# A Fourier image tokenizer before transformer blocks on one Trainium2 core: two scalings written ahead of an inverse root, and image and weight loads requested at other places

## The chip, the cores and the metric

The kernel runs on one core of a Trainium2 chip. The metric is device time in microseconds, lower is better. The engines that matter here are TensorE (PE in the profile, PEld its weight loads), VectorE (DVE), ScalarE (ACT), GpSimd (POOL) and SyncE (SP). SyncE does no arithmetic in this kernel: it waits for semaphores and requests DMA transfers, one after the other.

## The reference

64 images of 64x64 pixels with 3 channels go through a tokenizer, and the 64x64 result of every image through two small transformer blocks. The change touches only the tokenizer:

```
h = layer_norm(x @ fc0_w + fc0_b, ln0_g, ln0_b)          # 3 -> 32 channels
for i in range(4):
    x1 = spectral_conv(h, w1[i], w2[i])                  # rfft2, 2 x 12 x 12 modes mixed, irfft2
    x2 = einsum('bchw,oc->bohw', h, conv_w[i]) + conv_b[i]
    h = layer_norm(x1 + x2, ln_g[i], ln_b[i])            # over the 32 channels
    if i < 3: h = gelu(h)
h = gelu(h @ fc1_w + fc1_b); h = gelu(h @ fc2_w + fc2_b) # 32 -> 128 -> 64
return (h @ fc3_w + fc3_b)[..., 0]                       # 64 -> 1
```

After it come attention, a gated feed-forward net, a linear recurrence and a mixture of experts on the 64x64 hidden state. Neither the kernel before nor the changed one differs there.

## The kernel before, in words

**The loops.** The 64 images go through the tokenizer in 4 groups of 16 (`GROUPS`), and a group in 2 units (`u`) of 8 images. In a group there are five stages: stage 0 is the embedding, stages 1 to 3 are a hardware loop over layers (`l`), stage 4 is the last layer, and then comes the token head (`mlp`, fc1 to fc3). Each engine runs its own program over the same order, and semaphores tie them. Every stage and unit has one *main part*, so there are 4 x 5 x 2 = 40 of them: 8 embedding, 24 layer and 8 last ones. Behind the main part of stages 0 to 3 comes a *forward part* (`pe_forward`: transform along rows and columns, then the mixing with the weights in `mixw`).

**A main part** has 16 chunks of 512 columns. For chunk c, TensorE fills one of six PSUM banks (`wide`: four of `main`, two of `aux`) in L447 or in L454 and L457 and raises `main_full`. In the layers it does this for pairs of chunks: L454 writes the inverse transform of chunks c and c+1, and each needs its bank to be free, that is the scaling (`main_free`) of the chunk six before. ScalarE squares the bank (L730), VectorE sums the squares over the 32 channels (L708, `ssum`), 1/sqrt of the variance is made, and VectorE scales the bank with it into `xn` (L699, the function `scale`). TensorE transposes `xn` (L465, five chunks behind the filling, `LAG`), ScalarE applies gain, bias and GELU (L742), and in the layers TensorE and ScalarE turn the result once more (L473, L748).

**The inverse root** of a pair of chunks is made on VectorE by nine small dependent instructions (`newton_steps`, L659 to L676) for chunks 0 and 1, 2 and 3, 6 and 7, 10 and 11, 14 and 15, and on GpSimd by a power for the others (L762, L765). VectorE's program for a main part sums chunk c, then scales chunk c-3, then may do a Newton chain. `wait_rstd` is the wait for the root of the chunk that is to be scaled.

**SyncE's order** in one group is written by hand: wait for the start value of `main_full`, the images of both units (`sp_x`, 8 transfers and one of the embedding weights per unit, into `yd`), the spectra of both units (`sp_spectrum`: 8 stores to `y_scratch`, a wait for them, one load into `yd`), in the layer loop the next mixing weights (`sp_mixw`, 4.6 MB, one transfer) and two spectra, the first layer's mixing weights for the next group, and the stores of the tokens (`sp_tok`, 8 per unit), each behind the end of its unit's token head.

`yd` holds first a unit's images and later its spectrum. At a group's start TensorE waits for `x_in` before it transposes the images (`pe_embed`, L409), and VectorE and ScalarE wait for all token stores of the group before (`tok_out`, in `drain_embed`) before they copy those transposes out (L598); then TensorE starts the embedding main part (L447).

Of the kernel before, what the change touches and what calls it, by code (L numbers as in the profile page):

```python
# [15 lines left out]
LAYERS, M1, M2 = 4, 12, 12  # L16
GROUP, UNITS = 16, 2
GROUPS = IMGS // GROUP
# [5 lines left out]
NCH = S // 4  # L24
# [14 lines left out]
CHUNKS_GROUP = STAGES * UNITS * NCH  # L39
VAR_STEPS = {4: 3, 5: 3, 8: 3, 9: 3, 12: 2, 13: 2}  # L40

START = 1
# [65 lines left out]
def tokenizer(nc, t, tok, named):  # L108
# [9 lines left out]
    with ctx:  # L118
# [274 lines left out]
        def after(n, c, depth):  # L393

            return n + max(0, c - depth + 1)
# [297 lines left out]
        def dve_main(dve, g, s, u, l, nxt):  # L693
            m, _ = base_of(g, s, u, l)

            def scale(d):
                wait_rstd(dve, m, d)
                dve.wait_ge(tp_full, after(m, d, 2))
                dve.tensor_tensor(xn[:, d % 2, :].rearrange("p (n c) -> p n c", c=CH),  # L699
                                  wide[d % 6][:, :].rearrange("p (n c) -> p n c", c=CH),  # L700
                                  rstd[:, d % 4, :].unsqueeze(2).to_broadcast([128, 16, CH]),
                                  ALU.mult).then_inc(main_free, 1)

            for c in range(NCH):
                dve.wait_ge(sq_full, m + c + 1)
                if c >= 4:
                    wait_rstd(dve, m, c - 4)
                dve.tensor_reduce(ssum[:, c % 4, :], sq[:, c % 2, :].rearrange("p (n c) -> p n c", c=CH), AX.X,  # L708
                                  ALU.add).then_inc(red_done, 1)
                if c >= 3:  # L710
                    scale(c - 3)
                if c % 4 == 3 or c == 1:
                    dve_newton(dve, m, c)
            for d in range(NCH - 3, NCH):
                scale(d)
                if nxt is not None:
                    drain_inverse(dve, 0, g, *nxt, 2 * (d - NCH + 3))
            if nxt is not None:
                drain_inverse(dve, 0, g, *nxt, 6)
# [70 lines left out]
        def sp_x(sp, g, u):  # L790
            for b in range(NB):
                for a in range(NA):
                    img = g * GROUP + (u * UIMG + b * NA + a)
                    sp.dma_start(xb_of(u)[b:128:2, :].rearrange("r (k a n) -> r a k n", k=8, a=NA)[:, a],
                                 t["x"][bass.ds(img, 1)].rearrange("a r (k w) c -> r (a k) (w c)", k=8)).then_inc(x_in[u], 16)

            sp.dma_start(embw_of(u), embw_scratch).then_inc(x_in[u], 16)

        def sp_spectrum(sp, g, s, u, l):
            fwd = (g * (LAYERS * UNITS) + (0 if s == 0 else l * UNITS + UNITS) + u)  # L800
            sp.wait_ge(y_ready, fwd + 1)
            for half in range(2):
                for ro, ri, src in ((0, 0, ys), (0, 1, yn), (1, 0, ys), (1, 1, ys)):
                    part = ri if ro == 0 else 1 - ri
                    rows = 64 * half + 32 * part
                    dst = y_scratch[u].rearrange("(f x r o s m) -> f r s o x m", f=2, x=M1, r=2, o=CH, s=2)[half, ri, ro]
                    sp.dma_start(dst, src[rows:rows + 32, :].rearrange("o (x m) -> o x m", x=M1)).then_inc(y_stored, 16)
            sp.wait_ge(y_stored, fwd * 128 + 144)
            sp.dma_start(yd[0:96, u * YC:(u + 1) * YC], y_scratch[u].rearrange("(p n) -> p n", p=96)).then_inc(yd_in[u], 16)

        def sp_mixw(sp, layer):

            sp.dma_start(mixw[:, :], mix_scratch[bass.ds(layer, 1)].rearrange("a p n -> (a p) n")).then_inc(mixw_in, 16)
# [20 lines left out]
        with nc.Block() as block:  # L834
            @block.tensor
            def _(pe):
                def embed(g):
                    for u in range(UNITS):
                        nxt = (0, 0) if u == 1 else None
                        pe_embed(pe, g, u)  # L840
                        pe_main(pe, g, 0, u, None, nxt)
                        pe_forward(pe, g, 0, u, None, nxt)

                def layer(g, l):
                    for u in range(UNITS):
                        nxt = (1, l) if u == 0 else (0, l + 1)
                        pe_main(pe, g, 1, u, l, nxt)
                        pe_forward(pe, g, 1, u, l, nxt)

                def last(g):  # L850
                    for u in range(UNITS):
                        pe_main(pe, g, LAYERS, u, None, (1, LAYERS - 1) if u == 0 else None)

                def mlp(g):
                    for u in range(UNITS):
                        pe_mlp(pe, g, u)

                program(pe, embed, layer, last, mlp)

            def drains(eng, j, main_of, mlp_of):  # L860
                def embed(g):
                    for u in range(UNITS):
                        drain_embed(eng, j, g, u)
                        main_of(eng, g, 0, u, None, (0, 0) if u == 1 else None)
                        drain_forward(eng, j, g, 0, u, None)

                def layer(g, l):
                    for u in range(UNITS):
                        main_of(eng, g, 1, u, l, (1, l) if u == 0 else (0, l + 1))
                        drain_forward(eng, j, g, 1, u, l)  # L870

                def last(g):
                    for u in range(UNITS):
                        main_of(eng, g, LAYERS, u, None, (1, LAYERS - 1) if u == 0 else None)

                def mlp(g):
                    for u in range(UNITS):
                        mlp_of(eng, g, u)

                program(eng, embed, layer, last, mlp)  # L880

            @block.vector
            def _(dve):
                dve.memset(xs[:, :], 0.0).then_inc(xs_zero, 1)
                for i, counter in enumerate((*aux_full, *aux_free, *inv_full, *inv_free, *row_full, *row_free, turn_full, turn_free, main_full, main_free, sq_full, red_done, var_done, rstd_done, newton, early,
                                             tp_full, tp_free, fc1_full, g1_done, fc2_full, g2_done)):
                    dve.memset(start[:, i:i + 1], 0.0).then_inc(counter, START)
                dve.wait_ge(xs_zero, 1)
                drains(dve, 0, dve_main, dve_mlp)

            @block.scalar
            def _(act):
                for k in range(4):
                    act.wait_ge(p_store[k], 64 * LAYERS)
                act.dma_start(mixw[:, :], mix_scratch[0]).then_inc(mixw_in, 16)
                act.wait_ge(xs_zero, 1)
                drains(act, 1, act_main, act_mlp)

            @block.gpsimd
            def _(pool):  # L900
                def one(s):
                    def f(g, l=None):
                        for u in range(UNITS):
                            pool_main(pool, g, s, u, l)
                    return f
                program(pool, one(0), one(1), one(LAYERS), lambda g: None)

            @block.sync
            def _(sp):

                sp.dma_start(start_scratch[0:1, :], eps[0:1, :]).then_inc(y_stored, 16)
                sp.dma_start(start_scratch[1:2, :], eps[0:1, :]).then_inc(tok_out, 16)
                with sp.Fori(0, GROUPS) as g:

                    sp.wait_ge(main_full, g * CHUNKS_GROUP + START)
                    for u in range(UNITS):
                        sp_x(sp, g, u)
                    for u in range(UNITS):
                        sp_spectrum(sp, g, 0, u, None)
                    with sp.Fori(0, LAYERS - 1) as l:  # L920
                        for u in range(UNITS):
                            if u == 0:
                                sp_mixw(sp, l + 1)
                            sp_spectrum(sp, g, 1, u, l)
                    sp_mixw(sp, 0)
                    for u in range(UNITS):
                        sp_tok(sp, g, u)
                sp.wait_ge(tok_out, GROUPS * UNITS * TOK_DMAS * 16 + 16)
                sp.wait_ge(mixw_in, (GROUPS * LAYERS + 1) * 16)


N_SMALL = 16 + NA * (1 + 2 + 2 * LAYERS + 1) + 4
# [760 lines left out]
```

## Time and profile before

| | us |
|---|---|
| median of 3 runs (lowest, highest) | 4879.39 (4878.88, 4888.92) |
| the profiled execution, its own time | 4884.81 |
| its span in the trace | 4883.0 |
| PE busy | 3992.8 (82% of the span) |
| DVE busy | 2321.4 (48%) |
| ACT busy | 2100.9 (43%) |
| POOL busy | 809.0 (17%) |

A share of busy time is a mean over parts with different limits: preparation of the mixing weights until about 198 us, the four groups until about 4090 us, and the blocks behind them. A gap in square brackets in a row of the timeline is idle time of that engine before the row, with the instruction that ended it.

### The profile page before, as it was taken

What the parts mean: (1) busy time and instruction counts of PE and PEld (TensorE: products, weight loads), DVE (VectorE), ACT (ScalarE), POOL (GpSimd) and SP (SyncE); (2) the same over time, 40 slices, a digit from 0 to 9 for tenths busy, and PEclk for the clock granted to TensorE, in tenths of its full rate; (3) what the DMA queues carried; (4) which work ended last, traced back from release to release, by engine and by line L of the source; (5) the groups of instructions that cost most, each with busy time, mean ns of one, the idle gap of its engine ahead of it and who ended that gap; (6) DMA issues with size and microseconds to landing.
All of it is one profiled execution on the core that took longest, in us unless ns stands there. A gap on an engine that the chain in (4) does not pass through costs nothing. (4 is left out here: it accounts for less than half of the span.)

```text
span 4883.0 us, 102255 instructions
## 1 busy us (share of the span) xinstructions
PE 3992.8 (82%) x39344; PEld 3051.8 (62%) x39344; DVE 2321.4 (48%) x5028; ACT 2100.9 (43%) x3178; POOL 809.0 (17%) x540
## 2 busy tenths in 40 slices
PE   0189999996899999868999999699999995867268
PEld 0068788842687878427888783278888732753146
DVE  6554444531544445225444442244445422777666
ACT  1154444465544444654454446544444473221113
POOL 0031221310212112112121221112212210000020
PEclk9989999998899999989999999799999997778679
DMA  9501202200022021000210210002112101000000
GB/s 205 162 22 60 79 21 64 75 1 16 21 71 69 21 76 63 1 16 21 79 60 21 79 60 2 15 21 79 60 28 72 60 2 31 1 1 1 0 1 9
DMA packets 168694, 213.38 MB, mean 44 GB/s; under 512 B 156402, under 2 KB 158679, under 8 KB 159874
## 3 DMA queue, kind: packets, MB, share of 16 engines
q1 hardware_dynamic: 166514, 182.84, 12.8%
q10 hardware_dynamic: 1680, 23.60, 2.0%
q8 instruction: 347, 5.69, 0.5%
q14 instruction: 153, 1.25, 0.1%
HBM read 147.28 MB, written 59.12 MB: 42 GB/s over the span
## 5 line engine op out<-in xcount | busy, mean ns | idle before, releaser
L765 POOL TENSOR_TENSOR rstd<-var,mhalf 128x16 f32<-128x16 f32 x240 | 698.4, 2910 | 38.8 <-POOL var L762 17.1
L742 ACT ACTIVATE h<-tp,gb 128x512 f32<-128x512 f32 x640 | 554.0, 868 | 303.9 <-PE tp L465 301.9
L708 DVE TENSOR_REDUCE ssum<-sq 128x16 f32<-128x512 f32 x640 | 432.6, 683 | 453.7 <-ACT sq L730 451.3
L762 POOL TENSOR_TENSOR var<-ssum,eps 128x16 f32<-128x16 f32 x240 | 52.0, 217 | 3146.9 <-DVE ssum L708 3146.9
L457 PEld LDWEIGHTS main<-convw,h 128*128 128x128 f32 x3072 | 416.1, 213 | 164.8 <-issue 164.8
L465 PE MATMUL tp<-ident,xn 128*128 128x128 f32 x2560 | 438.7, 299 | 85.5 <-DVE xn L699 80.8
L730 ACT ACTIVATE sq<-main 128x512 f32<-128x512 f32 x480 | 286.4, 599 | 464.0 <-PE main L457 417.4
L506 PE MATMUL main<-fwd_w,pix 128*128 128x96 f32 x4096 | 464.8, 276 | 7.0 <-ACT pix L598 7.0
L506 PEld LDWEIGHTS main<-fwd_w,pix 128*128 128x128 f32 x4096 | 459.8, 192 | 10.3 <-DVE pix L598 8.7
L457 PE MATMUL main<-convw,h 128*128 (+1 forms) x3072 | 465.6, 304 | 0.0
L465 PEld LDWEIGHTS tp<-ident,xn 128*128 128x128 f32 x2560 | 324.1, 154 | 179.6 <-DVE xn L699 141.8
L424 PE MATMUL aux<-inv_r,yd 96*48 96x64 f32 x8192 | 420.0, 256 | 7.1 <-DVE zq L598 4.1
L424 PEld LDWEIGHTS aux<-inv_r,yd 96*48 96x48 f32 x8192 | 388.9, 185 | 46.3 <-issue 34.9
L454 PE MATMUL main<-zq,inv_w 48*128 48x512 f32 x768 | 290.1, 684 | 104.9 <-DVE xn L699 65.5
L699 DVE TENSOR_TENSOR xn<-main,rstd 128x512 f32<-128x512 f32 x480 | 326.9, 682 | 9.4 <-PE tp L465 9.4
L598 DVE COPY t_w<-main 128x384 f32<-128x384 f32 (+1 forms) x192 | 94.2, 491 | 473.5 <-PE main L506 392.7
L598 ACT COPY t_w<-main 128x384 f32<-128x384 f32 (+1 forms) x192 | 81.5, 425 | 505.8 <-PE main L506 405.2
L473 PE MATMUL tp<-ident,h 128*128 128x128 f32 x1536 | 240.0, 280 | 0.0
L748 ACT COPY pix<-tp 128x512 f32<-128x512 f32 x384 | 221.3, 576 | 19.2 <-PE tp L473 19.2
L598 DVE COPY zq<-aux 112x512 f32<-112x512 f32 x128 | 88.2, 689 | 265.5 <-PE aux L424 265.5
L573 PE MATMUL main<-h,f1w 32*128 32x512 f32 x1024 | 182.1, 672 | 14.1 <-ACT pix L773 9.6
L539 PE MATMUL main<-xs,mixw 128*64 128x32 f32 x6144 | 188.9, 223 | 0.0
(240 smaller groups left out, 5952.5 us busy)
## 6 DMA issues: line engine op xcount, KB each, us to landing
mixw<-mix_scratch SPq DMA_DIRECT2D x16, 4608.0 KB, 18.0
y_scratch<-t_w SPq DMA_DIRECT2D x256, 144.0 KB
yd<-y_scratch SPq DMA_DIRECT2D x32, 1152.0 KB, 7.3
mix_scratch<-mixw SPq DMA_DIRECT2D x64, 288.0 KB, 4.8
mixw<-mix_scratch ACTq DMA_DIRECT2D x1, 4608.0 KB, 13.8
h<-in_L_tok_w1r ACTq DMA_DIRECT2D x6, 576.0 KB, 9.7
h<-in_L_tok_w1i ACTq DMA_DIRECT2D x6, 576.0 KB, 10.1
h<-in_L_tok_w2r ACTq DMA_DIRECT2D x6, 576.0 KB, 18.6
```

The source lines that it names most:

```text
L424: mm = pe.matmul(aux[j][64 * half:64 * half + 48, 64 * i:64 * i + 64], ydv[:, u, 8 * e + i, :, :, a].rearrange("p s n -> p (s n)"), inv_r[ ...
L454: pe.matmul(wide[(c + half) % 6][:, :], inv_w[rows, :], zq[rows, 256 * c:256 * c + 512], start=True, stop=False)
L457: mm = pe.matmul(bank[:, 128 * i:128 * i + 128], h[:, (u * S + 4 * c + i) * 128:(u * S + 4 * c + i) * 128 + 128], convw[:, layer, :] if l ...
L465: mm = pe.transpose(tp[0 if turns else d % 2][:, 128 * i:128 * i + 128], xn[:, d % 2, 128 * i:128 * i + 128], ident[:, :])
L473: mm = pe.transpose(tp[1][:, 128 * i:128 * i + 128], h[:, (u * S + 4 * d + i) * 128:(u * S + 4 * d + i) * 128 + 128], ident[:, :])
L506: mm = pe.matmul(main[j][:, 48 * i:48 * i + 96], pv[:, c0 + i, 2 * ap:2 * ap + 2, :].rearrange("p a r -> p (a r)"), fwd_w[:, :], start=Tru ...
L598: return eng.tensor_copy(out, in_) if j == 0 else eng.copy(out, in_)
L699: dve.tensor_tensor(xn[:, d % 2, :].rearrange("p (n c) -> p n c", c=CH), wide[d % 6][:, :].rearrange("p (n c) -> p n c", c=CH), rstd[:, d ...
L708: dve.tensor_reduce(ssum[:, c % 4, :], sq[:, c % 2, :].rearrange("p (n c) -> p n c", c=CH), AX.X, ALU.add).then_inc(red_done, 1)
L730: act.activation(sq[:, c % 2, :], wide[c % 6][:, :], ACT.Square, scale=CH ** -0.5 / (CUBIC if c % 4 >= 2 or c < 2 else 1)).then_inc(sq_ful ...
L742: act.activation(out, in_, fn, bias=gb[:, 1, stage:stage + 1] if l is None else gb[:, 1, bass.ds(stage, 1)], scale=gb[:, 0, stage:stage + ...
L765: pool.tensor_tensor(rstd[:, c % 4, :], var[:, c % 4, :], mhalf[:, :], ALU.pow).then_inc(rstd_done, 2)
```

## The change

In VectorE's program the scalings of chunks 0 and 1 stand directly behind the sums of chunks 2 and 3. Before, they stood behind the sums of chunks 3 and 4. All later scalings stand where they stood.

In SyncE's program the images of group g+1 and the first layer's mixing weights for it are requested when the last main part of group g has filled its last bank, ahead of the token stores. The images of group 0 are requested without a wait. The mixing weights of layer l+1 are requested when the first unit's main part has filled eight banks. The last group requests neither images nor first mixing weights for a group to come.

```
-                if c >= 3:
+                if c in (2, 3):
+                    scale(c - 2)
+                if c >= 5:
                     scale(c - 3)
                 if c % 4 == 3 or c == 1:
                     dve_newton(dve, m, c)
...
-                with sp.Fori(0, GROUPS) as g:
-
-                    sp.wait_ge(main_full, g * CHUNKS_GROUP + START)
-                    for u in range(UNITS):
-                        sp_x(sp, g, u)
+
+                def layers(g):
                     for u in range(UNITS):
                         sp_spectrum(sp, g, 0, u, None)
                     with sp.Fori(0, LAYERS - 1) as l:
                         for u in range(UNITS):
                             if u == 0:
+                                sp.wait_ge(main_full, base_of(g, 1, 0, l)[0] + NCH // 2)
                                 sp_mixw(sp, l + 1)
                             sp_spectrum(sp, g, 1, u, l)
+                    sp.wait_ge(main_full, g * CHUNKS_GROUP + (START + CHUNKS_GROUP))
+
+                for u in range(UNITS):
+                    sp_x(sp, 0, u)
+                with sp.Fori(0, GROUPS - 1) as g:
+                    layers(g)
+                    for u in range(UNITS):
+                        sp_x(sp, g + 1, u)
                     sp_mixw(sp, 0)
                     for u in range(UNITS):
                         sp_tok(sp, g, u)
+                layers(GROUPS - 1)
+                for u in range(UNITS):
+                    sp_tok(sp, GROUPS - 1, u)
                 sp.wait_ge(tok_out, GROUPS * UNITS * TOK_DMAS * 16 + 16)
-                sp.wait_ge(mixw_in, (GROUPS * LAYERS + 1) * 16)
+                sp.wait_ge(mixw_in, GROUPS * LAYERS * 16)
```

VectorE's row at the start of a main part, before: the sums of chunks 2 and 3, the scaling of chunk 0, the first and last step of the Newton chain for chunks 2 and 3, and what follows it.

```order
L708 TENSOR_REDUCE ssum<-sq 128x16 [waits sq_full] x2
L699 TENSOR_TENSOR xn<-main,rstd 128x512 [waits tp_full,rstd_done]
L659 TENSOR_SCALAR var<-ssum 128x32 [waits red_done]
...
L676 SCALAR_TENSOR_TENSOR rstd<-newton_w,rstd 128x32 [waits newton]
L705 REGISTER_ALU
L708 TENSOR_REDUCE ssum<-sq 128x16 [waits rstd_done,sq_full]
L699 TENSOR_TENSOR xn<-main,rstd 128x512 [waits tp_full,rstd_done]
L708 TENSOR_REDUCE ssum<-sq 128x16 [waits rstd_done,sq_full]
L691 REGISTER_ALU
L699 TENSOR_TENSOR xn<-main,rstd 128x512 [waits tp_full,newton]
```

The same place in the changed kernel.

```order
L708 TENSOR_REDUCE ssum<-sq 128x16 [waits sq_full]
L699 TENSOR_TENSOR xn<-main,rstd 128x512 [waits tp_full,rstd_done]
L708 TENSOR_REDUCE ssum<-sq 128x16 [waits sq_full]
L699 TENSOR_TENSOR xn<-main,rstd 128x512 [waits tp_full,rstd_done]
L659 TENSOR_SCALAR var<-ssum 128x32 [waits red_done]
...
L676 SCALAR_TENSOR_TENSOR rstd<-newton_w,rstd 128x32 [waits newton]
L705 REGISTER_ALU
L708 TENSOR_REDUCE ssum<-sq 128x16 [waits rstd_done,sq_full] x2
L691 REGISTER_ALU
L699 TENSOR_TENSOR xn<-main,rstd 128x512 [waits tp_full,newton]
```

The scaling of chunk 0 moved ahead of one sum. That of chunk 1 moved ahead of the whole Newton chain and of one sum. From the scaling of chunk 2 on, the order is the same.

SyncE's row from the end of the layer loop to the tokens of unit 0, before:

```order
L920 REGISTER_ALU
L920 COMPARE_AND_BRANCH
L813 DMA mixw<-mix_scratch 128x9216
L818 ISA
L823 ISA [waits aux_free1,aux_free0]
L823 DMA tok<-pix 16x4x64
```

The same place in the changed kernel, with the repeated image transfers left out.

```order
L919 REGISTER_ALU
L919 COMPARE_AND_BRANCH
L925 ISA
L796 ISA [waits main_full]
L796 DMA yd<-in_x 64x8x24
...
L799 DMA yd<-embw_scratch 97x1024
L815 DMA mixw<-mix_scratch 128x9216
L820 ISA
L825 ISA [waits aux_free1,aux_free0]
L825 DMA tok<-pix 16x4x64
```

The 16 image transfers and two transfers of embedding weights, which before began the next turn of the group loop behind the token stores, now stand ahead of them, behind a wait for `main_full`.

## Rows read from the trace of the kernel before

**Rows 1.** The waits of the whole span: engine, line, releaser, us, times, longest.

```profile
PE aux L409 <- DMA yd<-embw_scratch: 152.2, 4, 55.7
```

**Rows 2.** Timeline of SP's requests at a group's end: start, us, queue, transfer, count.

```profile
1104.31 7.05 SPq L823 DMA_DIRECT2D tok<-pix  x8
1166.17 6.79 SPq L823 DMA_DIRECT2D tok<-zq  x8
1173.69 5.85 SPq L794 DMA_DIRECT2D yd<-in_x  x8
...
1180.26 19.54 SPq L794 DMA_DIRECT2D yd<-in_x  x8
```

**Rows 3.** Timeline of PE: last chunk of the group, then the next group's start.

```profile
1027.74 1.06 PE L457 MATMUL main<-convw,h 128*128 128x128 f32 x8
...
1197.70 1.94 PE L409 MATMUL aux<-ident,yd 128*96 128x128 f32 x8 [32.58 <-DMA yd<-embw_scratch]
1200.50 5.50 PE L447 MATMUL main<-yd 97*128 97x512 f32 x8 [0.86 <-ACT yd L598]
```

**Rows 4.** Timeline of ACT at the same group's start.

```profile
1174.65 1.28 ACT L598 ACT_TABLE_LOAD   x1 [10.74 <-DMA tok<-zq]
1199.68 0.58 ACT L598 COPY yd<-aux 96x512 f32<-96x512 f32 x1 [23.75 <-PE aux L409]
```

**Rows 5.** The waits of SP's queue, whole span.

```profile
SPq L794 <- DVE start L887: 4.7, 1, 4.7
```

**Rows 6.** Timeline of PE, first layer main part of group 0.

```profile
411.16 0.66 PE L465 MATMUL tp<-ident,xn 128*128 128x128 f32 x4 [0.85 <-DVE xn L699]
...
414.87 1.31 PE L454 MATMUL main<-zq,inv_w 48*128 48x512 f32 x2 [2.01 <-DVE xn L699]
...
421.26 1.13 PE L454 MATMUL main<-zq,inv_w 48*128 48x512 f32 x4
...
430.97 1.13 PE L454 MATMUL main<-zq,inv_w 48*128 48x512 f32 x4
```

**Rows 7.** Timeline of DVE, same main part.

```profile
409.23 1.28 DVE L708 TENSOR_REDUCE ssum<-sq 128x16 f32<-128x512 f32 x2
...
411.02 0.17 DVE L659 TENSOR_SCALAR var<-ssum 128x32 f32<-128x32 f32 x1
...
414.14 0.68 DVE L699 TENSOR_TENSOR xn<-main,rstd 128x512 f32<-128x512 f32 x1
...
415.33 0.68 DVE L699 TENSOR_TENSOR xn<-main,rstd 128x512 f32<-128x512 f32 x1
...
425.45 0.68 DVE L699 TENSOR_TENSOR xn<-aux,rstd 128x512 f32<-128x512 f32 x1
```

**Rows 8.** Timeline of ACT and POOL, same main part.

```profile
412.02 1.28 ACT L742 ACT_TABLE_LOAD   x1 [0.82 <-PE tp L465]
...
413.31 0.78 ACT L742 ACTIVATE h<-tp,gb 128x512 f32<-128x512 f32 x1
...
414.80 2.91 POOL L765 TENSOR_TENSOR rstd<-var,mhalf 128x16 f32<-128x16 f32 x1 [0.22 <-POOL var L762]
```

**Rows 9.** Windows: stretch, length, PE PEld DVE ACT POOL busy, PEclk, DMA, GB/s.

```profile
415.70:419.10 3.40, 3.40 (x15) 2.99 (x15) 0.56 (x2) 0.60 (x1) 3.18 (x3) 0.50 0.86 369
...
501.10:507.80 6.70, 6.70 (x28) 5.58 (x27) 1.92 (x4) 2.00 (x4) 5.43 (x3) 0.50 0.18 46
```

**Rows 10.** Idle time of PE before line L454, whole span: releaser, us, times.

```profile
  DVE xn L699: 67.6, 42
```

**Rows 11.** Timeline of DVE, chunk 7 of an embedding main part.

```profile
1297.38 0.69 DVE L708 TENSOR_REDUCE ssum<-sq 128x16 f32<-128x512 f32 x1 [1.16 <-ACT sq L730]
```

**Rows 12.** Mixing weights: landing (the page), one request, first use by PE.

```profile
mixw<-mix_scratch SPq DMA_DIRECT2D x16, 4608.0 KB, 18.0
...
410.02 0.38 SPq L813 DMA_DIRECT2D mixw<-mix_scratch  x1
...
479.26 0.42 PE L539 MATMUL main<-xs,mixw 128*64 128x32 f32 x8
```

## The prediction

> **What bounds the kernel now.** I read the list of waits first, to see what TensorE stands still for. Its largest entry that this change touches is the wait for images at the start of a group: 152.2 us in four times, the longest, at the very start, 55.7 us [rows 1]. The other three make about 32 us each. Then I read the timelines of SyncE, TensorE and ScalarE around one such place, and last the timelines of all engines through the first 20 us of one layer main part. There the reader is to see two things: from chunk 8 on TensorE has hardly a gap, so the main part goes at TensorE's pace, but at its beginning TensorE stands still for the scalings of chunks 0 and 1. The idle time before L454, which needs the scaling of chunk 1 for its second bank, is 67.6 us in 42 times [rows 10]; at 2.01 us a time [rows 6] the 32 layer and last main parts make 64 of it.
>
> **Images ahead of the tokens.** Now SyncE requests the tokens of unit 1 at 1166.17, is through at 1172.96, and only then begins with images. TensorE's transposes start at 1197.70 after 32.58 us idle, and the embedding proper at 1200.50, when ScalarE's copy is out [rows 2 to 4]. In the changed kernel the images are requested when the last chunk is in its bank, near 1029 [rows 3]. One unit took 24.0 us from request to transposes (1173.69 to 1197.70); the second's requests alone lasted 19.5 us. I give both 50 us and the weights 18 us [rows 12]: all has landed before 1104.31, when the first token stores go out [rows 2]. So SyncE's tokens are not late either. What is late next is the wait for the token stores in `drain_embed`: it ended at 1174.65, where ScalarE then loaded a table for 1.28 us before its copy [rows 4]. TensorE's transposes, 1.94 us, fit in the idle time before it. So the copy runs from 1175.95 to 1176.53, and the embedding starts 0.24 us later (1200.50 less the end of the copy, 1200.26), at 1176.77. That is 23.7 us earlier, three times: **71 us**.
>
> At the very start SyncE waited 4.7 us for VectorE's start values [rows 5], and TensorE waited for the images. That wait is gone, but the images then run longer beside the first load of mixing weights. Between 0 and 4.7 us I take **3 us**, nearer to the upper end, since TensorE waits for nothing else there.
>
> **Mixing weights in mid-loop.** One load takes 18.0 us. The request moves from 410.02 to about 417, and the first use is at 479.26 [rows 12]: 44 us of slack, in which the main part's second half and the transforms lie. Cost 0. Without that cover it would be 18 us twelve times. The load for a fifth group, which goes away, was hidden by other work: 0. Behind the new waits on SyncE stand only spectra that become ready later in the same stage.
>
> **Scalings of chunks 0 and 1.** I replay the main part of [rows 6 to 8] with its own durations. VectorE starts a sum or a scaling every 0.60 us when nothing is missing, and the Newton chain of chunks 2 and 3 runs from 411.02 to the sum of chunk 4 at 413.54, 2.52 us. New order: sum 2 at 409.23, scaling 0 at 409.83, sum 3 at 410.42, scaling 1 at 411.02 instead of 414.14, chain 411.62 to 414.14, sums 4 and 5 at 414.14 and 414.74, scaling 2 at 415.33. The work is the same, so scaling 2 stands where it stood. The price of the edit is that sum 4 is 0.6 us later, and with it GpSimd's root of chunk 4.
>
> TensorE: first transposes at 410.57 (was 411.16), L454 for both banks by 411.76 (was 414.87), chunk 6 done near 413.2. The transposes of chunk 1 then wait for ScalarE, which does its squares, loads the GELU table 1.28 us and activates 0.78 us: until 413.9. Chunk 7 is done at 415.85, chunk 2's transposes wait for scaling 2 until 416.3, and the next pair of L454 starts near 417.3. It was 421.26: 3.9 us. Not all of it stays. GpSimd's power takes 2.91 us and now ends near 418.3, so scaling 4 cannot start before 418.35; then comes the chain of chunks 6 and 7, and scaling 5 follows at about 422.1. It was at 425.45 [rows 7]: **3.3 us**. From there on the cycle of four chunks on VectorE (eight times 0.60 and 2.5 to 2.7 us, about 7.5) is shorter than TensorE's 9.7 (421.26 to 430.97 [rows 6]), so the lead stays to the end.
>
> The stall also costs clock. Behind it TensorE's granted clock is 0.50, its lower level of 1.2 GHz, for 3.4 us in this main part, and for 6.7 us in the next one [rows 9]. With only short waits left I expect that the clock does not fall there. In the replay the first 3.4 us are in; where it lasts twice as long, 1.1 to 1.7 us more come back. I take the mean of 3.3 and 4.4 us, 3.85, for 32 main parts: **123 us**.
>
> In the embedding VectorE itself sets the pace, and only its idle before the sum of chunk 7, 1.16 us [rows 11], can shrink. The later GpSimd root leaves 0.6 of it: eight times, **5 us**.
>
> A rule on the table: in 12 main parts (layer loop, first unit) it is loaded between the first scaling and the first activation, and in the new order TensorE waits for it. The rows show the activation at 413.31, directly behind a load of 1.28 us from 412.02 [rows 8]. By the Trainium skill, "ScalarE: Activation LUTs", What ACT_TABLE_LOAD costs, a switch costs 2.66 us with the drain; by that, 1.4 us more would be exposed twelve times and the sum would be 17 us smaller. The row shows no drain of that length before the activation, and the row decides.
>
> **The sum.** 71 + 3 + 123 + 5 = 202 us off the profiled execution's own time of 4884.8, which is 4682.8. The median of the runs is 5.4 us below that execution, so I predict 4678 us.
>
> **The rivals.** *Only the bare idle comes back.* The later sum 4 and GpSimd's root could hold VectorE so that of each of 32 main parts only the 2.01 us before L454 return. For it: these roots do come 0.6 us later. Against it: the replay has that in. It gives 64 + 71 + 3 = 138 us off, 4741 us. Chance 0.12.
>
> *The reordering does nothing.* Scaling 2 does not move, and if all of TensorE's order hung on it, only the loads would pay: 74 us, 4805 us. Against it: TensorE has eight matmuls of chunk 6 and more to do before it needs scaling 2. Chance 0.04.
>
> *The boundary keeps its wait.* If the token stores landed later behind the backlog of loads, or code for the next turn of the loop came late, up to 71 us would stay: 4749 us. Against it: 62 us lie between the two units' tokens [rows 2], with nothing else queued. Chance 0.05.
>
> *Slower.* The transfers that ran while TensorE stood still now run beside the token head (three times about 44 us), and the weights (12 times 18 us) in the dense middle of a main part. If instruction code of the engines comes through the same DMA engines, it could come late. TensorE would have to lose 201 of these 348 us, 58%, before the change costs anything; stopped for all of them, it would give 4878 + 147 = 5025 us. Against it: in the first half of this main part, with the weights under way at 369 GB/s, TensorE was busy for all 3.40 us [rows 9]. By the Trainium skill, "DMA: Bandwidth & Descriptors", Queues, rings and completion order, an engine takes turns between queues packet by packet, so a backlog on one queue would not shut out another. Chance 0.03.
>
> **How the numbers follow.** My forecast has 0.76, with a range of its own from 4655 (4.8 us per main part, and the embedding's clock better too) to 4715 (2.9 us per main part, which is 30 us less). The range has to reach the first rival: up to 4742, which leaves out 0.12 above and a few in 100 below. About 0.2% is what a measurement can tell from no change. Faster 0.96, same 0.01, slower 0.03.
>
> **What would show it.** In the trace after, TensorE's idle before L409 is near 0 at the group starts, and ScalarE's copy there follows its table load; the wait before it is for the tokens. The idle before L454 falls from 67.6 us to under 15. Scaling 5 comes about 12.9 us behind sum 2 of a layer main part (it was 16.2: 409.23 to 425.45), and windows of clock 0.50 behind chunk 7 are gone. I would be wrong above all if the clock still fell there, or if another wait, for GpSimd's root or for the two sums before scaling 5, took more than the replay gives it.

## The result, and the profile after

| | before | changed |
|---|---|---|
| median of 4 runs, us | 4881.36 | 4680.34 |
| ratio, 95% interval | | 0.9586, 0.957 to 0.9603 |
| the profiled execution, us | 4884.81 | 4677.02 |
| its span | 4883.0 | 4675.2 |

The kernel is 201 us faster: 4680.34 us, where 4678 were forecast. One of the six executions of the last experiment below ran slow, 6644.67 us at a mean granted clock of 0.629, and its ratio leaves that one out.

The waits of the changed kernel over the whole span, columns as in [rows 1]: engine, line, releaser, us, times, longest.

```profile
PE aux L409 <- DMA yd<-embw_scratch: 55.5, 1, 55.5
ACT L598 <- DMA tok<-zq: 32.2, 3, 10.8
PE aux L409 <- issue: 9.2, 3, 3.2
```

TensorE's wait for images is left at one place of four, the very start. At the other three it is gone, and what ends last there is the wait for the token stores, three times 10.8 us on ScalarE. That wait was there before too (32.1 us in three times), under the longer one for the images.

The requests of SyncE at the end of group 0 in the changed kernel.

```profile
995.99 5.76 SPq L796 DMA_DIRECT2D yd<-in_x  x8
1001.79 0.47 SPq L799 DMA_DIRECT2D yd<-embw_scratch  x1
1002.45 19.09 SPq L796 DMA_DIRECT2D yd<-in_x  x8
1021.59 0.46 SPq L799 DMA_DIRECT2D yd<-embw_scratch  x1
1022.09 3.41 SPq L815 DMA_DIRECT2D mixw<-mix_scratch  x1
1070.96 7.01 SPq L825 DMA_DIRECT2D tok<-pix  x8
1132.83 6.75 SPq L825 DMA_DIRECT2D tok<-zq  x8
```

The timeline of the changed kernel behind it, at the start of group 1. The first row is the last activation of the token head.

```profile
1129.44 1.11 ACT L780 ACTIVATE xn<-tp,fb 128x1024 f32<-128x1024 f32 x1 [2.12 <-PE tp L583]
...
1134.74 1.94 PE L409 MATMUL aux<-ident,yd 128*96 128x128 f32 x8 [2.98 <-issue]
1141.39 1.28 ACT L598 ACT_TABLE_LOAD   x1 [10.83 <-DMA tok<-zq]
1141.42 0.69 DVE L598 COPY yd<-aux 96x512 f32<-96x512 f32 x1 [8.84 <-DMA tok<-zq]
1142.68 0.58 ACT L598 COPY yd<-aux 96x512 f32<-96x512 f32 x1
...
1143.50 6.89 PE L447 MATMUL main<-yd 97*128 97x512 f32 x8 [6.82 <-ACT yd L598]
```

The transposes stand 2.98 us behind the head and wait for nothing that the profile shows; the prediction expected TensorE's idle time here to be near 0. Their copies wait for the tokens. From the tokens' first request to the first embedding matmul it is 10.67 us (1132.83 to 1143.50). Before it was 34.33 (1166.17 to 1200.50 in [rows 2, 3]): 23.7 us less.

The same layer main part as in [rows 6 to 8], in the changed kernel, engines mixed in order of time.

```profile
408.41 0.69 DVE L708 TENSOR_REDUCE ssum<-sq 128x16 f32<-128x512 f32 x1
409.01 0.68 DVE L699 TENSOR_TENSOR xn<-main,rstd 128x512 f32<-128x512 f32 x1
409.61 0.67 DVE L708 TENSOR_REDUCE ssum<-sq 128x16 f32<-128x512 f32 x1
409.75 0.66 PE L465 MATMUL tp<-ident,xn 128*128 128x128 f32 x4 [0.26 <-DVE xn L699]
410.20 0.68 DVE L699 TENSOR_TENSOR xn<-main,rstd 128x512 f32<-128x512 f32 x1
410.33 1.73 PE L454 MATMUL main<-zq,inv_w 48*128 48x512 f32 x4
...
414.51 0.68 DVE L699 TENSOR_TENSOR xn<-main,rstd 128x512 f32<-128x512 f32 x1
414.58 2.91 POOL L767 TENSOR_TENSOR rstd<-var,mhalf 128x16 f32<-128x16 f32 x1 [0.22 <-POOL var L764]
...
416.50 1.13 PE L454 MATMUL main<-zq,inv_w 48*128 48x512 f32 x4
...
417.53 0.69 DVE L699 TENSOR_TENSOR xn<-aux,rstd 128x512 f32<-128x512 f32 x1 [0.47 <-POOL rstd L767]
...
421.25 0.68 DVE L699 TENSOR_TENSOR xn<-aux,rstd 128x512 f32<-128x512 f32 x1
```

L454 for both banks of the third pair is one row without a gap, where before 2.01 us of idle time cut it in two. Its four matmuls take 1.73 us and those of the next pair 1.13, so a short wait for scaling 1 can still be inside the row. The next pair's L454 comes 8.1 us behind sum 2 (408.41 to 416.50); before it was 12.0 (409.23 to 421.26). Scaling 4 (417.53) waits 0.47 us for GpSimd's root, and scaling 5 stands 12.84 us behind sum 2, where 12.9 was forecast and 16.2 was before.

The prediction also said that the stretches of low clock behind chunk 7 would be gone. Two windows of the changed kernel at those places, in the first and the second layer main part; PEclk, the third number from the end, was 0.50 in [rows 9] and is 1.00 here.

```profile
415.40:418.80 3.40, 3.29 (x23) 2.40 (x24) 2.72 (x7) 2.15 (x5) 3.18 (x3) 1.00 0.91 304
498.00:504.00 6.00, 6.00 (x45) 4.85 (x45) 4.34 (x15) 4.75 (x9) 4.95 (x3) 1.00 0.02 4
```

Idle time of TensorE before L454 over the whole span, in the changed kernel; [rows 10] has the same view.

```profile
  DVE xn L699: 6.7, 12
```

Windows over all four groups up to the last scaling, first of the kernel before.

```profile
236.80:3936.60 3699.80, 3357.51 (x35056) 2627.63 (x35055) 1616.53 (x3967) 1801.49 (x2783) 746.59 (x480) 0.93 0.15 44
```

And of the changed kernel. Columns: length, PE PEld DVE ACT POOL busy, granted clock, DMA share, GB/s.

```profile
236.10:3732.70 3496.60, 3267.77 (x35056) 2560.45 (x35055) 1615.62 (x3967) 1791.65 (x2784) 747.37 (x480) 0.97 0.16 45
```

The stretch is 203.2 us shorter. TensorE does the same 35056 matmuls and is busy 89.7 us less; its idle time (length less busy) fell from 342.3 to 228.8, by 113.5 us. So less than half of what the trace gained is shorter matmuls: the mean granted clock rose from 0.93 to 0.97, while DVE's and POOL's busy time did not change by more than 1 us.

The same by kind of main part. A window here runs from the start of chunk 0's sum to the end of chunk 15's transposes, and each number is the sum over all main parts of its kind.

| us | before: length, TensorE busy | changed: length, TensorE busy |
|---|---|---|
| 24 layer main parts | 1209.96, 1156.45 | 1115.81, 1102.49 |
| 8 last main parts | 365.11, 328.06 | 335.53, 305.49 |
| 8 embedding main parts | 320.95, 251.95 | 314.91, 241.31 |

The 32 layer and last main parts are 123.7 us shorter: 47 us of it is idle time and 77 us is shorter matmuls. The granted clock was 0.93 to 0.97 in each of the 24 layer windows before, and it is 1.00 in every one of them now. The last main parts of the first unit are at 1.00 too (0.93 to 0.96 before), those of the second unit at 0.94 or 0.95 (0.88 to 0.95 before). The embedding parts are 6.0 us shorter together.

### The profile page after: what moved, and what is told of

Its sections match the earlier page's. It is cut to its first block and busy times, and to the rows that moved or that the text cites. A ratio compares the mean times of both kernels' runs of the same rounds, so it can differ in the third digit from the quotient of the medians.

```text
span 4675.2 us, 102193 instructions
## 1 busy us (share of the span) xinstructions
PE 3900.5 (83%) x39344; PEld 2983.1 (64%) x39344; DVE 2320.5 (50%) x5028; ACT 2091.3 (45%) x3178; POOL 809.9 (17%) x540
## 5 line engine op out<-in xcount | busy, mean ns | idle before, releaser
L465 PE MATMUL tp<-ident,xn 128*128 128x128 f32 x2560 | 418.2, 289 | 104.2 <-DVE xn L699 86.2
L457 PEld LDWEIGHTS main<-convw,h 128*128 128x128 f32 x3072 | 378.5, 196 | 150.4 <-issue 150.4
L465 PEld LDWEIGHTS tp<-ident,xn 128*128 128x128 f32 x2560 | 304.0, 147 | 198.3 <-DVE xn L699 170.9
L457 PE MATMUL main<-convw,h 128*128 (+1 forms) x3072 | 426.3, 287 | 0.0
L454 PE MATMUL main<-zq,inv_w 48*128 48x512 f32 x768 | 248.8, 656 | 40.1 <-issue 38.3
```

The costliest lines, as they stand in the source:

```text
L454: pe.matmul(wide[(c + half) % 6][:, :], inv_w[rows, :], zq[rows, 256 * c:256 * c + 512], start=True, stop=False)
L457: mm = pe.matmul(bank[:, 128 * i:128 * i + 128], h[:, (u * S + 4 * c + i) * 128:(u * S + 4 * c + i) * 128 + 128], convw[:, layer, :] if l ...
L465: mm = pe.transpose(tp[0 if turns else d % 2][:, 128 * i:128 * i + 128], xn[:, d % 2, 128 * i:128 * i + 128], ident[:, :])
```

## The experiments

Every time is a median, beside a median of the kernel before on the same chip: 4884.52 for the first four, 4881.19 for the next four, 4882.01 for the last two. The changed kernel ran beside one of 4881.36, so comparisons with it go best by the ratios.

**The order alone.** The kernel before with only this:

```
-                if c >= 3:
+                if c in (2, 3):
+                    scale(c - 2)
+                if c >= 5:
                     scale(c - 3)
```

> The kernel before with VectorE's new order alone, SyncE's program as before. My theory: the order and the requests act at different places, so the gains add: about 131 us of the 201 belong to the order (125 in the 32 layer and last main parts, 6 in the embedding), which gives about 4750 us. Rival (they share one gain, because less idle in the main parts comes partly from the moved weights): clearly above 4765 us.

Measured 4759.66 us, ratio 0.9744 (0.9729 to 0.9758): 125 us less. That is 10 us above my 4750, and below the 4765 of the rival. The granted clock of the 24 layer main parts rose to 0.99 or 1.00 in this kernel too. The idle before L454 fell from 67.6 to 5.8 us without any change of SyncE's program:

```profile
  DVE xn L699: 5.8, 11
```

**The requests alone.** The changed kernel with the old order on VectorE and without the mid-loop wait:

```
-                if c in (2, 3):
-                    scale(c - 2)
-                if c >= 5:
+                if c >= 3:
                     scale(c - 3)
...
-                                sp.wait_ge(main_full, base_of(g, 1, 0, l)[0] + NCH // 2)
```

> The images and first mixing weights requested ahead of the tokens, VectorE's order as before, the mixing weights of the next layer requested at once as before. My theory: 23 us at each of three group starts, under 1 us at the very start: about 4811 us. Rival (the token head suffers from transfers beside it and gives some of it back): above 4825 us.

Measured 4814.52 us, ratio 0.9855 (0.984 to 0.987): 70 us less. The two parts alone give 125 and 70, 195 us together, and both at once gave 201. With intervals of some 7 us either way on each, the two add up within the noise, and neither part needs the other.

**Mixing weights at once.** The changed kernel less the wait for half of the main part:

```
                             if u == 0:
-                                sp.wait_ge(main_full, base_of(g, 1, 0, l)[0] + NCH // 2)
                                 sp_mixw(sp, l + 1)
```

> The changed kernel with the mixing weights of the next layer requested at once again, without the wait for half of the main part. My theory: the transfer is hidden in both places, 4680 us, within 0.2%. Rival (at the head of the loop the transfer delays code or the spectrum, and the new place pays): 12 times 1 to 3 us more, 4692 us or above.

Measured 4681.81 us, ratio 0.9582 (0.9568 to 0.9595), against 0.9586 of the changed kernel. The new place neither costs nor pays. In this kernel the request stood at the head of the loop again (408.44, in the changed kernel 415.39), and the other waits of L454 stayed (40.3 us in 12 times that the profile puts down to nothing it shows, 38.3 in the changed kernel), so these gaps at the head of the layer loop are not this transfer's.

**Scaling 0 alone.** The changed kernel with scaling 1 back behind the chain:

```
-                if c in (2, 3):
-                    scale(c - 2)
-                if c >= 5:
+                if c == 2:
+                    scale(0)
+                if c >= 4:
                     scale(c - 3)
```

> The changed kernel with only the scaling of chunk 0 moved ahead by one sum; that of chunk 1 stands behind the Newton chain and sum 4 as before. My theory: the second bank of the third pair waits for scaling 1, which stays late, so nearly the whole gain of the order is lost: 4800 to 4812 us. Rival (each of the two moves brings a part of its own, as both end a wait of TensorE): near 4745 us.

Measured 4819.69 us, ratio 0.9867 (0.9852 to 0.9882). That is the time of the requests alone, if anything 5 us more, and outside my range of 4800 to 4812 by 8 us. Its timeline shows why there is a small loss:

```profile
410.67 1.12 PE L454 MATMUL main<-zq,inv_w 48*128 48x512 f32 x2
...
413.85 0.68 DVE L699 TENSOR_TENSOR xn<-main,rstd 128x512 f32<-128x512 f32 x1
...
414.59 1.43 PE L454 MATMUL main<-zq,inv_w 48*128 48x512 f32 x2 [2.80 <-DVE xn L699]
```

TensorE begins the pair 0.6 us earlier (1.93 us behind the start of sum 2 at 408.74; before it was 2.51, 409.23 to 411.74) and then stands still 0.8 us longer (2.80 against 2.01 in [rows 6]). The row of the kernel before, for the same two matmuls:

```profile
411.74 1.12 PE L454 MATMUL main<-zq,inv_w 48*128 48x512 f32 x2
```

The second bank is even later, 5.85 us behind sum 2 where it was 5.64, because scaling 1 is: 5.11 us (408.74 to 413.85) against 4.91 (409.23 to 414.14 in [rows 7]). If all 32 main parts lose these 0.2 us, that is an estimate of 6 us, which fits the 5 measured; both are within the noise. The whole idle before L454 rose from 67.9 us in the kernel with the requests alone to 82.8. Here a release that came earlier gained nothing, since the next one that the same engine needs did not.

**Both scalings behind sum 3.** The changed kernel with scaling 0 about half a microsecond later, where it also stood in the kernel before, and scaling 1 in its new place:

```
-                if c in (2, 3):
-                    scale(c - 2)
+                if c == 3:
+                    scale(0)
+                    scale(1)
```

> The changed kernel with both scalings behind sum 3, ahead of the chain: scaling 0 comes 0.6 us later than in the changed kernel, scaling 1 at the same time. My theory: it is scaling 1 ahead of the chain that pays, and GpSimd's root of chunk 4 sets scaling 4 in both: 4680 to 4690 us. Rival (the first transposes and what hangs on them, the GELU table load, are the critical step, 0.6 us in 32 main parts): 4700 us.

Measured 4683.68 us, ratio 0.9595 (0.9581 to 0.9608). The whole gain of the order is there without the move of scaling 0. It is scaling 1 ahead of the Newton chain that pays.

**Sums 4 and 5 ahead of the chain.** The changed kernel, with the chain of chunks 2 and 3 behind sum 5 and scaling 2 behind it:

```
-                if c >= 5:
+                if c > 5:
                     scale(c - 3)
-                if c % 4 == 3 or c == 1:
+                if c % 4 == 3 and c != 3 or c == 1:
                     dve_newton(dve, m, c)
+                if c == 5:
+                    dve_newton(dve, m, 3)
+                    scale(2)
```

> The changed kernel with the sums of chunks 4 and 5 also ahead of the Newton chain of chunks 2 and 3; scaling 2 directly behind the chain, at the same time as before. My theory: scaling 4 waits for GpSimd's root of chunk 4 (0.47 us idle in the trace), which now starts 2.5 us earlier, so each of 32 main parts gains about 0.5 us and each embedding 0.6 us: about 4660 us. Rival (TensorE or ScalarE sets the pace there, not the root): 4680 us.

Measured 4658.19 us, ratio 0.9541 (0.9528 to 0.9554): 22 us better than the changed kernel. The root of chunk 4 starts right behind its sum:

```profile
408.37 1.27 DVE L708 TENSOR_REDUCE ssum<-sq 128x16 f32<-128x512 f32 x2
...
409.63 2.91 POOL L770 TENSOR_TENSOR rstd<-var,mhalf 128x16 f32<-128x16 f32 x1 [0.22 <-POOL var L767]
...
412.13 0.69 DVE L699 TENSOR_TENSOR xn<-main,rstd 128x512 f32<-128x512 f32 x1
...
414.52 0.68 DVE L699 TENSOR_TENSOR xn<-aux,rstd 128x512 f32<-128x512 f32 x1
```

Scaling 4 (414.52) now comes 2.4 us behind scaling 2 (412.13); in the changed kernel it was 3.0 (414.51 to 417.53) with the wait for GpSimd in it. The half microsecond is the wait for the root that the replay in the prediction had. In the waits of the changed kernel it is this row, and in this experiment the row is gone:

```profile
DVE xn L699 <- POOL rstd L767: 20.3, 40, 0.7
```

The 20.3 us are close to the 22 gained. The edit moved the sums of chunks 4 and 5 as well, though, and ScalarE's wait for sums before its squares fell from 122.2 us in 85 times to 50.3 in 48. The two effects were not taken apart, so it is not shown that the root alone brings the 22 us.

**The token wait a main part later.** The changed kernel with

```
 def drain_embed(eng, j, g, u):
     _, n = base_of(g, 0, u)
-    if u == 0:
-        eng.wait_ge(tok_out, g * (UNITS * TOK_DMAS * 16) + 16)
...
 def drain_forward(eng, j, g, s, u, l):
...
     if s == 0:
+        if u == 0:
+            eng.wait_ge(tok_out, g * (UNITS * TOK_DMAS * 16) + 16)
```

> The changed kernel with the wait for the token stores moved from before the embedding's copies to before the first writes into the token buffers, a whole main part later. My theory: at each of three group starts VectorE's and ScalarE's copies no longer wait for the stores and follow the transposes, which start 3 us after the token head's end because of code; the embedding starts about 6 us earlier: 18 us, 4662 us. Rival (another wait takes its place, or stores beside the embedding cost): 4680 us.

Measured 4665.06 us, ratio 0.9553 (0.9538 to 0.9568): 15 us less than the changed kernel, about 5 us at each of three starts, where 6 was forecast. The start of group 1 in this kernel:

```profile
1133.20 1.11 ACT L780 ACTIVATE xn<-tp,fb 128x1024 f32<-128x1024 f32 x1 [2.12 <-PE tp L583]
1135.93 1.28 ACT L598 ACT_TABLE_LOAD   x1 [1.62 <-issue]
1140.15 0.58 ACT L598 COPY yd<-aux 96x512 f32<-96x512 f32 x1 [2.93 <-PE aux L409]
```

The copy now waits for TensorE's transposes, and the embedding's first matmul stood at 1140.97: 7.8 us behind the start of the head's last activation, 14.1 in the changed kernel.

**Images ahead of the first mixing weights.** The changed kernel with one wait more on ScalarE, before its load of the first mixing weights:

```
+                act.wait_ge(x_in[0], (UIMG + 1) * 16)
                 act.dma_start(mixw[:, :], mix_scratch[0]).then_inc(mixw_in, 16)
```

> The changed kernel with the very first load of mixing weights (4.6 MB, on ScalarE's queue) requested only when the images of unit 0 have landed. My theory: the images were requested 5.6 us earlier and landed only 0.6 us earlier because they ran beside this load; alone they take about 24 us, as at the later group starts, which gives 9 us less: 4671 us. Rival (the images' own 512 small pieces per transfer set their time): 4680 us.

Measured 4671.58 us, ratio 0.957 (0.9556 to 0.9585): 9 us less than the changed kernel, as forecast, though the two intervals overlap. The trace is clearer: TensorE's first transposes started at 220.54, where it was 230.51 in the changed kernel.

```profile
197.39 5.33 SPq L796 DMA_DIRECT2D yd<-in_x  x8
```

```profile
220.54 1.94 PE L409 MATMUL aux<-ident,yd 128*96 128x128 f32 x8 [45.49 <-DMA yd<-embw_scratch]
```

The first unit's images took 23.2 us from request to transposes without the 4.6 MB beside them, and 32.9 us (197.61 to 230.51) with them.

The records of the DMA packets in the traces show what happens meanwhile. The images go in packets of 96 bytes, the mixing weights in packets of 36864 bytes. From 206 to 208 us of the changed kernel there are 24 packets of images and 24 of mixing weights: one for one, whatever their size. From 200 to 202 us of this experiment, with no mixing weights under way, there are 1569 packets, nearly all of images. So the images all but stand still until the large load is through, at 210.5 us in the changed kernel.

**Images twice.** The changed kernel, where the images and embedding weights of the next group are requested a second time beside the token head, when the first have landed. TensorE's wait for them in `pe_embed` is adapted to the doubled count:

```
-                    for u in range(UNITS):
-                        sp_x(sp, g + 1, u)
+                    for twice in range(2):
+                        for u in range(UNITS):
+                            if twice:
+                                sp.wait_ge(x_in[u], g * (2 * (UIMG + 1) * 16) + 2 * (UIMG + 1) * 16)
+                            sp_x(sp, g + 1, u)
```

> The changed kernel with the images and embedding weights of the groups to come requested twice beside the token head, the second time when the first has landed. It doubles the suspected cost of transfers beside the token head. My theory: the token head does not feel them and there are still some microseconds to spare before the first token stores, 4680 us within 0.3%. Rival (transfers beside work slow it): whatever they cost now comes a second time, above 4695 us.

Measured 4682.1 us, ratio 0.9592 (0.9578 to 0.9606): no difference that can be told from noise. The requests of SyncE in it:

```profile
1040.01 19.47 SPq L796 DMA_DIRECT2D yd<-in_x  x8
1059.53 0.46 SPq L799 DMA_DIRECT2D yd<-embw_scratch  x1
1060.03 2.88 SPq L815 DMA_DIRECT2D mixw<-mix_scratch  x1
1070.01 25.02 SPq L825 DMA_DIRECT2D tok<-pix  x8
1131.88 6.73 SPq L825 DMA_DIRECT2D tok<-zq  x8
```

The first tokens' requests stood behind this backlog and took 25.02 us instead of 7.01. Even so they were through 37 us before the second tokens' (1095.03 to 1131.88).

**The three that paid, together.** The changed kernel with the edits of sums 4 and 5, the token wait, and the images first.

> The changed kernel with the three edits that paid by themselves: sums 4 and 5 ahead of the chain, the token wait a main part later, the first mixing weights behind the first images. My theory: they act at different places and add up, 22 + 16 + 9 us: about 4633 us. Rival (the earlier embedding start meets the token stores, or the start of the next stage takes the gain back): 4645 us or above.

Measured 4635.92 us, ratio 0.9495 (0.9482 to 0.9507). That is 44 us better than the changed kernel, against 22 + 15 + 9 = 46 for the three by themselves. It is the fastest version that was run, and 3 us from the 4633 that I expected.

## Why the prediction was right

**Images ahead of the tokens, 71 us.** Right in mechanism and size. The trace gives 23.7 us at the start that was worked out, and the requests alone gave 70 us, where 71 and 3 were forecast. What comes late next was also as forecast, the token stores; moving that wait away gave 15 us more.

**The very start, 3 us.** Mis-sized: it was 0.6 us. The request came 5.6 us earlier (203.19 in the kernel before, 197.61 in the changed one), but TensorE's transposes only 0.6 us earlier (231.14, then 230.51). The step that failed is the choice "nearer to the upper end": the prediction named the load of mixing weights beside the images and then priced it too low. The run with the images first shows what that load costs, 10.0 us of the start.

**Mixing weights in mid-loop, 0.** Right; without the wait the time was 4681.8 us.

**Scalings, 123 us, and the embedding, 5 us.** Together 128, measured 125 in the run with the order alone. By the table of main parts the two terms are 123.7 and 6.0 us. The replay was also right in its single places: it has GpSimd's root let scaling 4 start at 418.35 and scaling 5 follow at 422.1, which is 9.12 and 12.9 us behind sum 2, and the changed kernel shows 9.12 (408.41 to 417.53) and 12.84. The step that carried it, that the second bank of the third pair waits for scaling 1 and for nothing else, was shown by two runs: scaling 0 alone gives nothing, and scaling 1 gives all. The bound that the replay named for scaling 4, GpSimd's root, shows as a wait in the trace and is gone where the root starts earlier.

**The table load.** ScalarE's activation at 412.29 in the changed kernel stands directly behind a load that starts at 410.99, and the sum held without the 17 us that a longer switch would have cost. The row decided rightly.

**The clock.** The prediction expected the lower level to vanish behind chunk 7, and it did: all 24 layer windows are at 1.00. Of the 89.7 us of shorter matmuls 77 belong to the 32 main parts. The prediction's 3.3 to 4.4 us per main part held both idle and clock and did not separate them, so only their sum was tested, 3.85 us against 3.87 measured. Of these 1.5 us are idle time, though the wait before L454 alone shrank by 1.9 (67.6 to 6.7 us over 32 parts): other waits grew, TensorE's wait for ScalarE before the transposes for one, from 4.1 to 17.0 us. That the middle of the range was met to 0.02 us is partly luck, since the choice of its mean rested on two main parts.

**The arithmetic.** Two bounds do not follow from their reasons: 4.8 us per main part gives 4648 us and not 4655, and 2.9 us gives 4708 and not 4715. The sum itself gives 4677.4, where 4678 stands. Nothing hangs on it here.

**The rivals.** *Only the bare idle* (138 us off) and *the reordering does nothing* (74 us off) fell with the run of the order alone. *The boundary keeps its wait* fell with the trace. *Slower*: doubling the transfers beside the token head changed nothing beyond noise, and the 29.5 us of requests that now start each group's loads (995.99 to 1025.50) went unfelt. From its first matmul to the last tokens' request, the first token head takes 127.7 us (1005.17 to 1132.83); before it was 128.0 (1038.18 to 1166.17).

Two arguments against *slower* were weaker than they read. TensorE was busy for all 3.40 us beside 369 GB/s, but at a clock of 0.50, where its work takes longer. The changed kernel has a better row: busy 3.29 of 3.40 us beside 304 GB/s at a clock of 1.00. And packets of two queues do take turns, as the prediction has it; but turns of one packet each held the small images to 24 packets in 2 us beside the mixing weights. That cost 10 us at the very start. Beside the token head the loads of a group all stand in SyncE's queue, so that case does not arise there.

## What to carry to other kernels

Where a hand-written order puts a chain of small dependent instructions between a buffer's release and the engine that waits for the buffer, move the release ahead of the chain, and look for the last of the releases that one consumer needs: moving only the first gained nothing here. Ask what else the delayed work starts (here another engine's 2.9 us root) and put that ahead of the chain too. Loads whose target buffer is free long before they are needed belong in the queue ahead of stores that come late; then look at what the next wait is, since here it was a wait that protected a buffer not written until a main part later.

## What the runs showed of the hardware that was not expected

A stall of 2 us in every main part cost more than itself. In the 32 layer and last main parts TensorE's idle time fell by 47 us, and its busy time for the same matmuls by 77 us, with the granted clock of the layer main parts going from 0.93 to 0.97 up to 1.00. One scaling written ahead of nine small instructions did nearly all of that, as the run with both scalings behind sum 3 shows.

Requesting a transfer of small pieces earlier, beside a large one, hardly moved its landing. The transposes that wait for the first images, requested 5.6 us earlier, started 0.6 us earlier; with the large load held back they started 10.0 us earlier still. The two queues took turns packet by packet, 24 of 96 bytes and 24 of 36864 bytes in 2 us, where the small ones alone came to more than 1500 in 2 us.
